# Routing the first expert layer pair by pair inside the first attention, with second choices stored apart and appended by copies in memory

## What is computed

```python
x = x + tanh(g_xattn[0]) * L0_attention(layernorm(x), ctx, ctx, mask)   # 16 heads of 16
x = x + tanh(g_ffn[0])   * L0_experts(layernorm(x))                     # this change
x = x + tanh(g_xattn[1]) * L1_attention(layernorm(x), ctx, ctx, mask)   # 16 heads of 64
x = x + tanh(g_ffn[1])   * L1_experts(layernorm(x))
```

```python
exp_mask = transpose(one_hot(top_i, 8), (1, 0, 2))       # first choices of all tokens, then second
exp_rank = cumsum(exp_mask.reshape(2 * T, 8), axis=0) - 1
exp_mask = exp_mask * (exp_rank < cap)
h = gelu(expert_rows @ c_fc); out = weights * (h @ c_proj)
```

## Time and profile before

| | us |
|---|---|
| three runs | 1683.36, 1679.73, 1685.15 (median 1683.36) |
| the profiled execution | 1681.74, of which its span is 1679.9 and 1.84 lie around it |
| first attention, steady iteration of one pair | 40.0 |
| end of the first attention to the first expert's first matmul | 377.65 to 469.35 |
| the eight experts' matmuls | 469.35 to about 669 |
| second attention | about 740 to 1375 |

### The profile page before, as it was taken

How to read it: one execution, slowest core, us unless ns; L and a number is a source line. 1 busy time by engine, 2 the same in 40 slices (tenths; PEclk the granted TensorE clock), 3 DMA queues, 4 the chain that set the end, 5 groups by cost and what they waited for, 6 DMA issues and landing times. The chain is left out here.

```text
span 1679.9 us, 35318 instructions
## 1 busy us (share of the span) xinstructions
PE 1311.7 (78%) x10632; PEld 1041.5 (62%) x10633; DVE 869.0 (52%) x2918; ACT 810.1 (48%) x2219; POOL 308.4 (18%) x337
## 2 busy tenths in 40 slices
PE   3699999984089998059999999999999973049970
PEld 2576676664078888057787878787878753026650
DVE  3466666664035544446665656665665656302223
ACT  3588778773044543136554555555545544013320
POOL 2333333310700000711000000000000000430016
PEclk9899999995589999569999999999999995579995
DMA  5811000000232320220000000000000000822113
GB/s 138 346 29 27 26 26 26 27 2 0 78 139 100 134 104 26 74 83 11 21 11 11 10 10 10 10 10 10 10 10 0 1 1 0 319 60 66 62 58 107
DMA packets 42626, 92.25 MB, mean 55 GB/s; under 512 B 10205, under 2 KB 30877, under 8 KB 39261
## 3 DMA queue, kind: packets, MB, share of 16 engines
q1 hardware_dynamic: 32468, 77.37, 13.6%
q0 software_dynamic: 8192, 13.15, 2.8%
q10 hardware_dynamic: 1872, 0.68, 0.3%
HBM read 66.18 MB, written 24.97 MB: 54 GB/s over the span
## 5 line engine op out<-in xcount | busy, mean ns | idle before, releaser
L507 ACT ACTIVATE b_prob<-b_prob,b_low 100x361 f32<-100x361 f32 x256 | 155.6, 608 | 108.0 <-DVE b_low L596 108.0
L364 PE MATMUL b_ps_p<-b_context_part,b_wk_part 128*128 128x362 f32 x768 | 157.7, 342 | 0.0
L1046 ACT ACTIVATE a_prob<-a_prob,a_low 100x361 f32<-100x361 f32 x256 | 154.2, 605 | 4.4 <-DVE a_low L1164 4.4
L515 ACT COPY b_prob_t<-b_ps_t 128x300 f32<-128x300 f32 x256 | 103.8, 406 | 104.2 <-PE b_ps_t L420 101.3
L370 PE MATMUL b_ps_p<-b_wv_part,b_context_part 128*128 128x512 f32 (+1 forms) x576 | 151.6, 406 | 0.0
L596 DVE CUSTOM_DVE_ANT_0 b_prob<-b_ps_s,b_mask_bias 100x361 f32<-100x361 f32 x256 | 121.3, 532 | 45.3 <-PE b_ps_s L410 30.0
L1164 DVE CUSTOM_DVE_ANT_0 a_prob<-a_ps_s,a_mask_bias 100x361 f32<-100x361 f32 x256 | 121.5, 532 | 34.8 <-PE a_ps_s L947 34.8
L420 PE MATMUL b_ps_t<-ident,b_prob 100*128 100x100 f32 x768 | 117.1, 261 | 22.1 <-ACT b_prob_t L515 21.5
L1054 ACT COPY a_prob_t<-a_ps_t 128x300 f32<-128x300 f32 x256 | 97.7, 409 | 67.7 <-PE a_ps_t L957 64.8
L364 PEld LDWEIGHTS b_ps_p<-b_context_part,b_wk_part 128*128 128x128 f32 x768 | 124.6, 189 | 0.3 <-issue 0.2
L420 PEld LDWEIGHTS b_ps_t<-ident,b_prob 100*128 100x128 f32 x768 | 78.1, 141 | 66.3 <-issue 52.4
(11 more groups left out here) (205 smaller groups left out, 2530.5 us busy)
## 6 DMA issues: line engine op xcount, KB each, us to landing
rows_in<-zero SPq DMA_DIRECT2D x16, 512.0 KB, 13.9
w<-in_c_fc SPq DMA_DIRECT2D x8, 1024.0 KB, 6.3
w<-in_c_proj SPq DMA_DIRECT2D x8, 1024.0 KB, 4.9
f_w<-in_W SPq DMA_DIRECT2D x2, 4096.0 KB
a_context<-in_ctx SPq DMA_DIRECT2D x16, 361.0 KB, 3.6
b_context<-in_ctx SPq DMA_DIRECT2D x16, 361.0 KB
f_xe<-rows_in SPq DMA_DIRECT2D x8, 512.0 KB, 3.9
rows_out<-f_ye SPq DMA_DIRECT2D x8, 512.0 KB, 3.0
```

The source lines that it names most:

```text
L364: ins = nc.tensor.matmul(bank[:, 0:LN2], w_parts["k"][a][:, k, t * P:(t + 1) * P], cx_parts[s][b][:, k, :], start=m == 0, stop=m == DK * l ...
L507: nc.scalar.activation(prob[0:S, k, 0:L], prob[0:S, k, 0:L], ACT.Exp, bias=low[0:S, k:k + 1], scale=-1.0, accum_out=total[0:S, k:k + 1]).t ...
L515: nc.scalar.copy(pt[:, k % PAIR_PT, :], ps_t[:, 0:KT_N * S]).then_inc(pt_ready.sem, 1)
L1046: nc.scalar.activation(prob[0:S, k, 0:L], prob[0:S, k, 0:L], ACT.Exp, bias=low[0:S, k:k + 1], scale=-1.0, accum_out=total[0:S, r:r + 1]).t ...
```

## The change

The separate normalisation `n1_`, the routing on DVE over all 16 batches and the 32 scatters after it are gone for the first expert layer. A new class `Router` does them for two batches at a time, inside `attention_first`, one iteration behind the attention:

- The W unit of batch 1 of the pair before moves from slot 4 to slot 3. In slot 4 DVE aggregates the moments (`moments`), POOL makes scale and shift by powers (`scales`, 4 instructions) and ACT normalises two batches (`make_rows`).
- New units: N in slot 5 (four transposes, a DVE copy), G in slot 6 (logits; DVE copies them and runs `choose`: maxima, indices, one-hots), C in slot 7 (two count matmuls, a DVE copy). In slot 7, after C, POOL runs `route` (16 small instructions, most of which wait for the one before) and `scatter` (4 indirect DMAs). A unit "none" in slot 4 keeps the number of units even.
- In the last iteration the same three units follow for the last pair in slots 12 to 14.
- POOL's loop over pairs is unrolled, and POOL waits ahead of it until rows_in of this layer is cleared.
- First choices of expert e go to rows from 1024 e, second choices to a second region from 8192 + 1024 e, each counted on its own. When all are counted, SP reads the number of first choices of an expert and copies the 512 second-choice rows behind them, memory to memory (`append`, 512 KB), ahead of each expert's row load. `load_later` clears 16 blocks of 512 KB for this layer in place of 8, besides 8 for the other, and in this order ahead of the expert weights.
- `experts_first` is `feed_forward` with n = 0 otherwise unchanged: expert loop, gather, combine. The second expert layer is unchanged.

```diff
     def __call__(self, eng):
         eng.sem_inc(self.sems[eng.engine], 1)
+
+
+EXPONENTS = (-0.5, 0.5, -1.0)
...
+    def scales(self, pool, j):
+
+        g, r = self.nc.gpsimd, slice(0, S)
+        if j:
+            pool.wait_ge(self.dispatched, 64 * j)
+        pool.wait_ge(self.averaged.sem, self.averaged.at(j, 1))
+        self.pool_own.link(pool, g.tensor_scalar(self.rs[r, :], self.mv[r, :, 1], LN_EPS, None, ALU.add))
+        self.pool_own.link(pool, self.power(self.rs, -0.5))
+        self.make_shift(pool, self.scaled)
+
+    def make_rows(self, act, j):
+
+        act.wait_ge(self.scaled.sem, self.scaled.at(j, 1))
+        self.apart(act)
+        for s in range(2):
+            ins = self.nc.scalar.activation(self.rows[0:S, s * D:(s + 1) * D], self.T["x"][0:S, bass.ds((2 * j + s) * D, D)],
+                                            ACT.Identity, scale=self.rs[0:S, s:s + 1], bias=self.shift[0:S, s:s + 1])
+        ins.then_inc(self.rowed.sem, 1)
...
+    def choose(self, dve, j):
+
+        v = self.nc.vector
+        dve.wait_ge(self.routed.sem, self.routed.at(j, 0))
+        self.apart(dve)
+        v.max(self.best[0:S, 0, :], self.lg[0:S, 0, :])
+        self.own.link(dve, v.max(self.best[0:S, 1, :], self.lg[0:S, 1, :]))
+        self.apart(dve)
+        r = slice(0, S)
+        v.max_index(self.where[r, 0, :], self.best[r, 0, :], self.lg[r, 0, :])
+        self.own.link(dve, v.max_index(self.where[r, 1, :], self.best[r, 1, :], self.lg[r, 1, :]))
+        self.own.link(dve, v.tensor_copy(self.pick[r, :, :].rearrange("p k b -> p b k"), self.where[r, :, 0:2]))
+        for k in range(2):
+            ins = v.tensor_tensor(self.hot[r, k, :, :], self.T["experts"][r, :].unsqueeze(1).to_broadcast((S, 2, E)),
+                                  self.pick[r, k, :].unsqueeze(2).to_broadcast((S, 2, E)), ALU.is_equal)
+        if self.n:
+            self.own.link(dve, ins)
+            ins = v.tensor_tensor(self.either[r, :, :], self.hot[r, 0, :, :], self.hot[r, 1, :, :], ALU.add)
+        ins.then_inc(self.hot_ready.sem, 1)
...
+    def route(self, pool, j):
+
+        g, r, run, rank, own = self.nc.gpsimd, slice(0, S), self.T["run"], self.rank, self.pool_own
+        if self.n == 0:
+            shape = dict(k=2, b=2, e=E)
+            within, tot = (self.counts[:, m * 32:(m + 1) * 32].rearrange("p (k b e) -> p k b e", **shape) for m in range(2))
+            own.link(pool, g.tensor_tensor(run[:, :, 1, :], run[:, :, 0, :], tot[:, :, 0, :], ALU.add))
+            own.link(pool, g.tensor_tensor(rank[r, :, :, :], within[r, :, :, :], run[r, :, :, :], ALU.add))
+            own.link(pool, g.tensor_tensor(rank[r, :, :, :], rank[r, :, :, :], self.hot[r, :, :, :], ALU.mult))
...
+            g.tensor_tensor(run[:, 0, 0, :], run[:, 0, 1, :], tot[:, 1, :], ALU.add)
+        for w in (4, 2, 1):
+            dst = rank[r, :, :, 0:w] if w > 1 else self.rank_of[r, :, :].unsqueeze(3)
+            own.link(pool, g.tensor_tensor(dst, rank[r, :, :, 0:w], rank[r, :, :, w:2 * w], ALU.add))
+        g.tensor_copy(self.T["picked"][r, :, 2 * j:2 * j + 2], self.rank_of[r, :, :])
+        if self.n == 0:
+            first = 2 * E * self.STRIDE + 4 * S * j
+            g.tensor_scalar(self.ok[r, :, :], self.rank_of[r, :, :], float(CAP), None, ALU.is_lt)
+            own.link(pool, g.tensor_scalar(self.row[r, :, :], self.pick[r, :, :], float(self.STRIDE), float(-first), ALU.mult, ALU.add))
+            own.link(pool, g.tensor_tensor(self.row[r, :, :], self.row[r, :, :], self.rank_of[r, :, :], ALU.add))
+            own.link(pool, g.tensor_tensor(self.row[r, :, :], self.row[r, :, :], self.T["offset"][r, :, :], ALU.add))
+            own.link(pool, g.tensor_tensor(self.row[r, :, :], self.row[r, :, :], self.ok[r, :, :], ALU.mult))
+            own.link(pool, g.tensor_scalar(self.row[r, :, :], self.row[r, :, :], float(first), None, ALU.add))
+        else:
+            own.link(pool, g.tensor_scalar(self.row[r, :, :], self.pick[r, :, :], float(REGION), None, ALU.mult))
+        last = self.T["unique"] if self.n == 0 else self.rank_of
+        own.link(pool, g.tensor_tensor(self.row[r, :, :], self.row[r, :, :], last[r, :, :], ALU.add))
+        own.link(pool, g.tensor_copy(self.scat[r, :, :], self.row[r, :, :]))
+        pool.sem_inc(self.routed.sem, 1)
...
+    def scatter(self, pool, rows_in):
+
+        for k, s in [(k, s) for k in range(2) for s in range(2)]:
+            pool.indirect_dma_start(out=rows_in[:, :], in_=self.rows[0:S, s * D:(s + 1) * D], in_offset=None,
+                                    out_offset=bass.IndirectOffsetOnAxis(ap=self.scat[0:S, k, s:s + 1], axis=0)
+                                    ).then_inc(self.dispatched, 16)
 
...
     at[0].append(("W", 0, 0, -1))
     at[1] += [("K", 1, 0, 0), ("V", 1, 0, 0)]
     at[2] += [("R", 1, 0, -1), ("V", 1, 1, 0)]
-    at[3] += [("K", 1, 1, 0), ("V", 1, 2, 0)]
-    at[half].append(("W", 1, 0, -1))
+    at[3] += [("K", 1, 1, 0), ("V", 1, 2, 0), ("W", 1, 0, -1)]
+    at[ROUTE_AT + 1].append(("N", 0, 0, -1))
     at[half + QUAD_VALUE].append(("R", 0, 0, 0))
...
+    at[ROUTE_AT + 2].append(("G", 0, 0, -1))
     if last:
-        at[half + QUAD_VALUE + 1].append(("W", 0, 0, 0))
+        at[half + QUAD_VALUE + 1] += [("W", 0, 0, 0), ("C", 0, 0, -1)]
         at[QUADS + QUAD_VALUE].append(("R", 1, 0, 0))
         at[QUADS + QUAD_VALUE + 1].append(("W", 1, 0, 0))
...
     at[5] += [("K", 0, 0, 0), ("Q", 0, 0, 0)]
     at[6] += [("V", 0, 0, 0), ("V", 0, 1, 0)]
-    at[7] += [("K", 0, 1, 0), ("Q", 0, 1, 0), ("V", 0, 2, 0)]
+    at[7] += [("K", 0, 1, 0), ("Q", 0, 1, 0), ("V", 0, 2, 0), ("C", 0, 0, -1)]
     at = at[:QUADS]
-    assert sum(len(slot) for slot in at) % FIRST_BANKS == 0
+    for k in range(-sum(len(slot) for slot in at) % FIRST_BANKS):
+        at[ROUTE_AT].append(("none", 0, k, 0))
     return Units(layer, [u for slot in at for u in slot], at)
 
...
             def steps(i, sched):
-                for p in range(QUADS):
+                for p in range(len(sched.slots)):
                     if sched is full and p == half:
                         convert(0, i + 2, maxed.at(i, H))
                     for u, unit in sched.slots[p]:
                         if unit[0] in ("Q", "K"):
                             lower(unit, sched.split[u], i, False)
+                    j = routed_pair(i, p)
+                    if j is not None:
+                        router.scales(pool, j)
+                    for u, unit in sched.slots[p]:
+                        if no_outputs(i, unit[3]):
+                            continue
+                        if unit[0] == "G":
+                            router.note(pool, i + unit[3])
+                        elif unit[0] == "C":
+                            pool.wait_ge(taken.sem, taken.at(i, u + 1))
+                            router.route(pool, i + unit[3])
+                            router.scatter(pool, D_["xs0"])
                 if sched is full:
                     convert(1, i + 2, maxed.at(i, HEADS))
 
+            router.credit_pool(pool)
             lo_ready.credit(pool)
             half_lower.credit(pool)
             convert(0, 1, None)
...
-            iterations(pool, steps)
+            pool.memset(T["run"][:, :, :, :], 0.0).then_inc(zeroed, 1)
+            pool.wait_ge(zeroed, 6)
+            pool.wait_ge(D_["cleared"][0], D_["cleared_value"][0])
+            for i in range(PAIRS):
+                steps(i, full if i < PAIRS - 1 else final)
+            nc.gpsimd.tensor_scalar(T["have"][:, :], T["run"][:, 0, 0, :], float(SLOTS), None, ALU.min).then_inc(zeroed, 1)
+            pool.wait_ge(zeroed, 7)
+            nc.gpsimd.tensor_copy(T["firsts"][:, :], T["have"][:, :]).then_inc(router.summed, 1)
 
         @block.tensor
         def _(pe):
...
+            def append(e, s):
+
+                have = sp.value_load(T["firsts"][0:1, bass.ds(e, 1)], min_val=0, max_val=SLOTS)
+                sp.dma_start(XS[bass.ds(have + e * STRIDE, SLOTS), :].rearrange("(p j) d -> p (j d)", j=4),
+                             XS[bass.ds(e * STRIDE + E * STRIDE, SLOTS), :].rearrange("(p j) d -> p (j d)", j=4)
+                             ).then_inc(merged[s], 16)
+
+            def load_rows(e, s):
+                sp.dma_start(xe[s][:, :, :], X4[:, bass.ds(e, 1), 0, :, :].rearrange("p e j d -> p (e j) d")).then_inc(rows_in[s], 16)
+
+            def step(i, s, more, two):
...
+                if two:
+
+                    append(2 * i + s + 2, s)
+                    wait(sp, x_turned, i, s)
+                    apart(sp)
+                    sp.wait_ge(merged[s], 16 * (i + 2))
+                    apart(sp)
+                    load_rows(2 * i + s + 2, s)
+                    sp.wait_ge(w1_ready.sem, w1_ready.at(i, DK * s))
+                    apart(sp)
+                    sp.dma_start(w1[s][:, :, :], D_["c_fc"][bass.ds(2 * i + s + 2, 1), :, :, :].rearrange(
...
+            for s in range(2):
+                append(s, s)
```

(40 more changed lines are left out.)

977 lines of the change are left out of this document (586 added, 391 removed).

## The result

The changed kernel takes 1722.3 us (median of 4 runs, 1719.7 to 1725.0) against 1682.0 for the kernel before on the same chip: 1.0238 times as long, 95% interval 1.0211 to 1.0266. The forecast was 1719, range 1686 to 1750, slower with a chance of 0.84. The profiled execution took 1719.69, of which its span is 1717.9, 38.0 more than the span before.

The account below looks back on a forecast made before the run. PE bounds the kernel around the first expert layer, but waits between attention and experts. Tail -51, clears +10, POOL's order +54 and new units +24.5 make +37.5 on 1681.74: 1719 us, range 1686 to 1750.

Parts of the forecast that it names:

- POOL's order: Slot 7, iterations 2 to 7: route and scatters ahead of the mask conversion make DVE wait; 9.0 us a pair, +54.
- The slack: Old DVE idling at the keep-mask wait that isn't needed again: about 1.0 us of the 8.7 us wait.
- The clock: PE's granted clock falls behind each mask wait; 1.3 us a pair taken, up to 2.1.
- New units: Added N, G, C and row work in slots 3 to 7: 3.5 us a pair, +24.5 over 7 iterations.
- First iteration: Eight more clears, 4.2 MB, ahead of the next pair's context in SP's queue: +10.0 us, 9 to 11.
- One sign: Predicted sign in the timeline after: PE's idling in the first iteration 10 us longer.
- The tail: Last statistics to first up projection: only one pair left to route at the end, giving back 51 us, 45 to 56.
- rival 4: Tail not freed: POOL late with the pair before last, so `scales` waits longer; 0.14 together with the third rival.
- The port: Scatters beside busy DVE held up by the shared port; by rows 2.2 us a pair, 13 in all.
- Rival 3: Slower still: port, 1732; or a 3 us power on POOL stopping ACT and N, +9; 0.14 together with the fourth rival.
- Rival 1: Faster: POOL's block fits the old slack, small instructions 0.12 us apart, scatters at 1.0; 1663; chance 0.09.
- Its deciding point: The faster rival holds or fails at 2.75 us of net wait a pair behind POOL's block.

Follow-up runs that it names:

- e1: Changed kernel with POOL's slot-7 mask conversion put ahead of route and the four scatters; 1669.9 us, 0.9934 of the kernel before.
- e2: Changed kernel with only the four scatters put behind the mask conversion, route staying ahead of it; 1678.3 us.
- e4: Changed kernel with mask conversion ahead of route and scatters, and eight clears behind the first iteration's context loads; 1658.4 us, 0.9859 of before.
- e3: Changed kernel with the eight clears of the second layer's rows issued behind the first iteration's two context loads; 1712.05 us.
- e6: e5 with all 24 clears and the four expert weight loads behind the first iteration's two context loads; four runs, 1699.3 to 1725.2 us.
- e10: e4 with all clears and expert weight loads behind the first context loads, and POOL's wait for the cleared region ahead of the first scatter; 1661.4 us.
- e5: e4 with the output projection (W unit) moved from the end of slot 3 to its head, ahead of key and value units; 1681.7 us.
- e9: e5 with the 32 scatters left out, so rows are not stored; one execution, span 1643.3 us.
- e8: e4 with the output projection (W unit) in slot 3 between the key unit and the value unit; 1651.0 us, 0.9824 of before.

## Why the prediction came out right

- **POOL's order, forecast +54 (27 to 66): 51 to 52.** e1 gives 52.4 by the medians, 8.55 a pair by the traces, against 9.0. Its parts: `route` was put at 5.3 with 0.33 us from start to start; the trace has 4.6 us for the sixteen (0.29 from start to start on average, most of them 0.20 each at 4 columns) and 0.9 until the first scatter. `scatter` was put at 5.9, which counted 0.7 for its later start (the rows that it cites give 0.8); without that start it is 5.1. Together 10.6 against 11.2. The wait, 8.7, is 8.4 to 9.0 in the six. The slack was sized too small: 1.0 against the 1.8 that e2 shows (2.9 of wait, 1.1 of cost at the full clock). The clock made up for it: 1.3 was forecast, and the stretch behind the wait is 2.1 longer than e2's on average, 10.3 against 8.2.
- **New units, forecast 24.5 (14 to 35): about 27.** 3.9 a pair by e1 and e4, seven times, 3.0 to 3.2 in iterations with the full clock. By slots: 2.5 between 3 and 5 (forecast 2.0), 0.3 between 5 and 7 (1.0), 0.4 behind (0.5). The sum was right, the share of slot 6 too large, and short falls of the clock, which the forecast left out here, bring 0.7.
- **First iteration, +10.0 (9 to 11): 10.2** by e3, 12.0 in the two traces; the queue in front of the context was the place. One sign came out otherwise: PE's idling ahead of the K unit grew by 7.4 us (5.84 to 13.19) and not by 10, since PE's work ahead of it had ended 3.8 us later; PE goes on 11.1 us later than before.
- **The tail, -51 (-56 to -45): -50.1.** The chain stands in the trace link by link. `scales` start 4.0 us behind the last statistics (forecast 4.75; they wait 1.78 for the landing, so rival 4 was no case of its own), from there to `route` it is 9.3 (8.2), from `route` to SP's issue of the copy 14.9 (14.4), its landing takes 4.1 (5), the row load 4.4 (3.4, with two in flight), turning and splitting 4.7 (4.6): 41.6 against 40.35. Inside the 14.9 two errors cancel: POOL is done with its counts at 492.3, a us sooner than sized, but the next block of the program begins before SP issues, 4.0 us later (forecast 2.5 behind that point).
- **The port.** The forecast weighed a rule of the Trainium skill ("SBUF — State Buffer", section "SBUF: two separate sides"): GpSimd can't write the descriptors of its DMAs while VectorE runs an operation in a two-port mode. The forecast took it for any busy VectorE. The changed kernel can't try that: there DVE stands still while the 24 scatters of iterations 2 to 7 run (in the timeline above from 262.6 to 271.0), since it waits for the mask behind them. e1 can, where DVE is busy beside them. The view of the scatter's line and a window over four scatters:

```profile
L321 POOL DMA_INDIRECT rows_in<-a_rows,a_scat x32: 992/992/1283, 159.7 to 441.6; - x32
...
205.00:211.00 6.00, 5.55 (x88) 4.22 (x87) 4.70 (x18) 5.85 (x20) 4.86 (x5) 1.00 0.21 58
```

The median is 0.992 us with DVE busy 4.7 of 6 us, as in the quiet before, and the 1.28 is a first one of four. So what DVE runs there (maxima, takes and copies out of PSUM) didn't hold a scatter up. Whether any of it was in such a mode the trace doesn't show, so the rule itself wasn't put to the test. Rival 3 falls, in its other half too: a power takes 0.73 us, `scales` with the hand-over are 1.8 in place of 1.3, and ACT waits 0.16 us for them.
- **Rival 1**, faster, needed small instructions at 0.12 from start to start; they are 0.29. Its deciding point was a cost of 2.75 us a pair. The changed kernel's 8.55 lie above it; e2, with 2.9 of wait and about 1 of cost, lies below, and is 0.36% faster than before (0.9942 to 0.9986), as that sum says.

The forecast's mechanism was right. That its total came within 4 us was in part luck: the slack, too small by 0.8 us a pair, and the clock, too small by about as much, err in opposite ways. With a shorter wait, where the clock hardly counts, that shows: e2 was put 11 us above e1, and 8.4 came by the medians (the two profiled spans are 11.7 apart, of which 5.1 lie in the six periods). The forecast also put the wait at the top of the waits view, where it stands 13th: a sum over the kernel doesn't rank waits by what they cost.

## What to carry to other kernels

Small work put onto an engine that is 33% busy isn't free: ask what already stands in that engine's queue, who waits for it and when, and put the new work behind it; here that one line is 52 us. Before moving transfers out of the way, follow every wait on their semaphore, since one that was hidden comes up (e6), and move no more than fits ahead of the next load (e10). Price a wait from its slack on: 2.9 us of it cost about 1 a pair, 8.7 cost 8.55.

## What was not expected of the hardware

- In e5 signals of PE came up to 3.7 us behind the entered ends of their products in each of iterations 3 to 7, and DVE idled without a releaser in iteration 2, only while POOL issued indirect DMAs: e9, the same program without them, doesn't have it, and e8, with the same DMAs and one unit in another place of slot 3, doesn't either. e6, with e5's order, has it again. Which orders will have it can't be told from their programs, and the cause stays open. Its price is 4.3 us a pair, PE's lower clock behind it included (0.72 in the six us from 346).
- Tiny POOL instructions of the `route` chain start 0.29 us apart on average (0.19 to 0.35 us each for 4 to 32 columns), but a power over two columns is 0.73 us, and the first indirect DMA behind such a chain starts 0.92 us after it.
- A copy of 512 KB from memory to memory lands 4.1 us after its issue (median of eight), 0.8 later than a load of that size (3.3).
